# Fused decoder layer: the mirrored columns for the first join, and the place of X of level 0 in the round

## The reference, cut to what matters

```python
mixed = silu(conv4(x @ w_qkv)); z = x @ w_z          # q, k, v from mixed, q and k of unit length
def step(S, (q, k, v, g, b)):
    S = S * exp(g)
    delta = (v - k @ S) * b
    S = S + outer(k, delta)
    return S, q @ S                                   # o
on = rmsnorm(o * silu(z)) * norm_w
out = on @ w_out
```

## Time and profile before

| what | value |
|---|---|
| time, median of three runs | 3113.66 us (3106.82 to 3114.77) |
| the profiled execution | 3111.22 us, span 3109.4 us |
| mean granted TensorE clock | 0.978 |
| busy: TensorE, VectorE, ScalarE, GpSimd | 2949.2 us (95%), 2671.0 (86%), 1935.2 (62%), 634.4 (20%) |
| instructions: TensorE, VectorE | 29096, 6317 |
| DMA queue of the kernel | 454566 packets, 314.87 MB, 34.1% of 16 engines |
| from one `turn_kq` to the next | 38.7 (chunk 0), 42.9 (1), 42.5 (2), 39.8 us (3), as read in rounds 43 to 46 |

### The profile page before, as it was taken

The page is one execution under the profiler, slowest core; times in us unless marked ns, Lnnn a source line. Parts: engine busy times, 40 slices in busy tenths (PEclk is TensorE's granted clock), DMA queues, the critical chain, the costliest instruction groups (busy, mean ns, idle before and its releaser), DMA issues. The chain is left out here.

```text
span 3109.4 us, 79479 instructions
## 1 busy us (share of the span) xinstructions
PE 2949.2 (95%) x29096; PEld 2419.4 (78%) x29096; DVE 2671.0 (86%) x6317; ACT 1935.2 (62%) x6258; POOL 634.4 (20%) x911
## 2 busy tenths in 40 slices
PE   6999999999999999999999999999999999649998
PEld 3788888888888888888888888888888888536665
DVE  4798989898988889898989898889888888789984
ACT  4576666666767666666667666666676766533332
POOL 1121212121212121111212121112121211162320
PEclk9899999999999999999999999999999999859999
DMA  7433434333433343433343333333343333020000
GB/s 259 141 88 107 121 108 123 105 117 103 123 107 118 89 123 109 123 100 122 96 128 89 103 115 110 121 108 115 105 121 107 116 92 101 22 99 21 28 14 17
DMA packets 454952, 319.96 MB, mean 103 GB/s; under 512 B 244003, under 2 KB 407971, under 8 KB 436902
## 3 DMA queue, kind: packets, MB, share of 16 engines
q1 hardware_dynamic: 454566, 314.87, 34.1%
HBM read 247.26 MB, written 50.73 MB: 96 GB/s over the span
## 5 line engine op out<-in xcount | busy, mean ns | idle before, releaser
L1077 DVE SCALAR_TENSOR_TENSOR conv<-xb,convw,conv 128x512 f32<-128x512 f32 x768 | 591.6, 774 | 97.6 <-ACT conv L786 82.8
L569 PE MATMUL bank<-x_hi,w_hi 128*128 128x512 f32 x1024 | 429.4, 419 | 10.1 <-PEq L263 6.4
L569 PE MATMUL bank<-x_hi,w_lo 128*128 128x512 f32 x1024 | 402.9, 393 | 0.0
L569 PE MATMUL bank<-x_lo,w_hi 128*128 128x512 f32 x1024 | 400.2, 391 | 0.0
L780 ACT ACTIVATE xb<-bank 128x512 f32<-128x512 f32 x256 | 161.7, 632 | 302.5 <-PE bank L569 277.9
L581 PE MATMUL bank<-w_hi,x_hi 128*128 128x256 f32 x1024 | 303.1, 296 | 1.6 <-ACT conv L786 1.6
L581 PE MATMUL bank<-w_lo,x_hi 128*128 128x256 f32 x1024 | 289.6, 283 | 0.0
L581 PE MATMUL bank<-w_hi,x_lo 128*128 128x256 f32 x1024 | 289.6, 283 | 0.0
L1160 POOL TENSOR_TENSOR small<-small,half 128x4 f32<-128x4 f32 x64 | 64.5, 1008 | 1047.7 <-DVE small L904 1047.7
L1188 POOL COPY halo<-xb 128x12 f32<-128x12 f32 x256 | 93.3, 365 | 863.3 <-ACT xb L780 863.3
L569 PEld LDWEIGHTS bank<-x_hi,w_hi 128*128 128x128 f32 x1024 | 193.8, 189 | 47.4 <-issue 10.1
(11 more groups left out here) (266 smaller groups left out, 7644.5 us busy)
## 6 DMA issues: line engine op xcount, KB each, us to landing
x_hi<-x_hi_scratch SPq DMA_DIRECT2D x63, 1024.0 KB, 5.0
x_lo<-x_lo_scratch SPq DMA_DIRECT2D x63, 1024.0 KB, 8.2
E<-decay_scratch SPq DMA_DIRECT2D x64, 512.0 KB, 5.4
M_scratch<-M SPq DMA_DIRECT2D x128, 256.0 KB, 2.2
w_raw<-in_w_proj SPq DMA_DIRECT2D x64, 384.0 KB, 8.5
Mt<-M_scratch SPq DMA_DIRECT2D x256, 64.0 KB, 2.0
U<-Ut SPq DMA_DIRECT2D x256, 64.0 KB, 2.0
w_raw<-in_w_out SPq DMA_DIRECT2D x32, 256.0 KB, 2.9
```

The costliest lines, as they stand in the source:

```text
L569: mm = pe.matmul(banks[j % 2][:].rearrange("p (b t) -> p b t", b=B), lhsT=t[f"w_{p}"][:, k, j, :], rhs=t[f"x_{q}"][:, k], start=i == 0, st ...
L1077: dve.scalar_tensor_tensor(out=y3, in0=xb[:, :, i:i + C], scalar=t["convw"][:, j, i:i + 1], in1=y3, op0=ALU.mult, op1=ALU.add).then_inc(on ...
```

## The change

1. Mt. Each of the four loads L348 is cut to the 64 columns of its own half (the ones that levels 0 and 1 read). Four more loads bring, for rows q = 0 and 1, the column blocks 2 and 3 to the places 3 and 2, so that Mt's upper right part is mirrored by columns too. Together 160 instead of 96 counts of `d_M` a step.
2. `join_a` takes from Mt one product of 64 columns instead of two of 32: eight matmuls instead of twelve.
3. TensorE: `x_part(r+1, 0)` moves ahead of `gate(r+2, 2)`. VectorE: `turn_T(r+1, 0)` and `x_part(r+1, 0)` move ahead of `taps(r+2, 2)`.

```diff
-                sp.wait_ge(on["d_M"], 96 * s + 32)
+                sp.wait_ge(on["d_M"], 160 * s + 32)
...
                 for q in range(4):
-                    sp.dma_start(Mt[rows(3 - q)], M_units[rows(q), 4:8]).then_inc(on["d_M"], 16)
+                    own = slice(0, 64) if q < 2 else slice(64, 128)
+                    sp.dma_start(Mt[rows(3 - q), :, own], M_units[rows(q), 4:8, own]).then_inc(on["d_M"], 16)
+                for q in range(2):
+                    for k in (2, 3):
+                        sp.dma_start(Mt[rows(3 - q), :, rows(5 - k)], M_units[rows(q), 4:8, rows(k)]).then_inc(on["d_M"], 16)
...
-                pe.wait_ge(on["d_M"], 96 * (s + 1))
+                pe.wait_ge(on["d_M"], 160 * (s + 1))
...
                 pe.matmul(x64[hi, i], lhsT=M8[lo, i, hi], rhs=T64[lo, i, :], start=True, stop=True)
-                for q in (2, 3):
-                    mm = pe.matmul(x64[at(i + 4, q), i], lhsT=Mt[hi, i, rows(q)], rhs=T64[hi, i, :], start=True, stop=True)
+                mm = pe.matmul(x64[lo, i], lhsT=Mt[hi, i, hi], rhs=T64[hi, i, :], start=True, stop=True)
             mm.then_inc(on["XF"], 1)
...
                 gate(r + 2, 1)
+            if solve:
+                x_part(r + 1, 0)
+            if ahead:
                 gate(r + 2, 2)
-            if solve:
-                x_part(r + 1, 0)
...
                 taps(r + 2, 1, range(early, TAPS - 1))
-                taps(r + 2, 2)
             if solve:
                 turn_T(r + 1, 0)
                 x_part(r + 1, 0)
             if ahead:
+                taps(r + 2, 2)
                 taps(r + 2, 3, (0,))
```

More of the change, by code:

```diff
@@ L611, in tensor @@
                 gate(r + 2, 1)
-                gate(r + 2, 2)
             if solve:
                 x_part(r + 1, 0)
+            if ahead:
+                gate(r + 2, 2)
             if ahead:
```

## The result

The change takes the median from 3113.2 to 3096.1 us (ten runs each). The ratio of the changed kernel to the kernel before is 0.9947, with a 95% interval from 0.9922 to 0.9972: faster by 0.5%, where 0.9% was forecast. The single runs spread more than before, 3071 to 3111 us against 3106 to 3117.

What follows compares the result with a forecast made beforehand. TensorE sets the pace (busy 491 of 500 us), VectorE follows (445). Steps of -1.83 us per four rounds, 16 times, give -29; +1.4 once makes -28: 3083, or 3086 with 2.4 for the median. Range 3036 to 3119.

Steps and rivals of the forecast that it cites:

- The forecast steps: Shifts of the solve's start from each chunk's round to the next, together -1.83 us in four rounds.
- The join: `join_a` on TensorE falls from 1.95 to 0.62 us, 1.33 us less a round; ceiling 85 us in 64 rounds.
- VectorE's end hands over: At the round's end, TensorE's 1.33 us can't be taken out of any round unless VectorE's end moves too.
- a slack of 1.05 us at U: `turn_kq` of the next round waits for ScalarE's U, behind VectorE's last taps; slack 1.05 us, but 0.38 in chunk 1.
- The other hand-over, M: VectorE waits for the Gram product ahead of M, up to 0.6 us in chunks 1 and 3; lateness beyond about 0.8 delays the solve.
- Chunk 1: TensorE's 1.22 us wait for Xc goes, but VectorE's end comes only 0.33 us earlier, by its lost idle time.
- The loads at nothing: SP's four more Mt loads take about 1.9 us to issue, at no cost; 0.5 us likely enough for the range.
- the sign that I had named for a price: More than the present 5.1 us from T's save to the last of Tc's loads, and waits for Tc in all chunks.
- The new waits for Tc: About 1 us on both engines in chunks 3 and some of 0; in round 43, 1.4 us VectorE, 0.9 TensorE.
- A: Slacks at U and M don't bind, so the join's gain arrives whole: -73 us, 3041; chance 0.18.
- B: T's save or Tc's loads queue behind the later E, delaying every Tc: +10 us, 3124 at 1.2 us; chance of slower 0.14.
- C: The two joins don't overlap, `join_a` stays above 1.5 us, sum about zero: 3113; chance 0.18, shared with a gain-eating Tc delay.
- D: X earlier frees nothing since Y still waits for R from ScalarE; in chunk 1 costs 5 us of forecast; no chance given.

Runs made afterwards that it cites:

- U first: ScalarE's `join_b` ahead of v's second Silu: on the whole change 3089.6 us (0.9929); on the kernel with the moves in chunks 1 and 2 only 3057.3 us (0.9824).

## Why the prediction was right, and where not

**The number** lies within the range, at -17 us where -28 was forecast. Part of that is luck. The forecast steps for chunks 0 to 3 were -0.3, -0.33, -0.75 and -0.45 us; measured are +0.55, -1.19, -0.65 and +0.10. Chunk 2 alone came near its forecast. Chunks 0 and 3 have the wrong sign, and chunk 1 gained more than three times what I gave it.

**The join** was sized right: 0.62 us, as `join_b`. Four matmuls at the 0.12 us that I had read for one would have left it at about 1.5; I put the rest down to the tiles' width, which no longer alternates. No run changes the width and keeps the count, so this division is argued. The Trainium skill says in "TensorEngine Tiling (Array Packing)", Tiling Modes, Key Properties, that a change of the tiling mode drains TensorE; the rows agree: before, the two kinds start 0.23 to 0.26 us apart, and the matmuls of one kind now 0.06.

**That the join's gain arrives in part only** was right. 85 us of TensorE time became 31 to 33 us alone (0.9896) and 50 with the moves where they help. The reason I gave, that VectorE's end hands over, is shown for chunk 1 by U (15 waits, one in four rounds) and by what took U's place when U came earlier: another instruction at VectorE's end. For the other chunks I had read a slack of 1.05 us at U, under the 1.33; there U never shows as a wait, in no run. So in the sum the step from chunk 3 to 0 had the wrong limit: with the join alone, where TensorE waits only 5.0 us for Tc, that step is -0.56 us and not -1.05. The other hand-over, M, was used up as forecast: VectorE's waits for the Gram product go from 43 to 15. TensorE's and VectorE's waits for R, N and Y are there instead; which of them holds a round is not settled by these runs.

**Chunk 1** was sized too small. I counted 0.33 us of VectorE's idle time; the moves alone take 0.71 us off this chunk (42.88 to 42.17), and the join's share comes on top. Where the rest comes from was not followed.

**The loads at nothing** was right for the loads by themselves. But the sign that I had named for a price is there in part: in round 43, from T's save to the last of Tc's issues, 5.7 us against 5.1, and in chunk 0 Tc comes 0.9 us later in the round with the loads alone. What that adds to the new waits is not measured.

**The new waits for Tc** were placed right: VectorE's are in chunks 3 and 0 alone, and so are 40.2 of TensorE's 41.1 us (the two others, of 0.49 and 0.37 us, are in chunks 1 and 2). They were put too small. In chunks 0 and 3 the join alone gained 0.75 and 0.56 us; with the waits and the drops behind them both got longer. Their size: I had 0.9 us on TensorE for round 43 and found 1.77:

```profile
1896.84 0.45 PE L431 MATMUL bank<-Tc,M 32*32 32x32 f32 x32 [1.77 <-issue]
```

In that round SP needed 6.2 us from T's save (1889.25) to the end of Tc's issues, against 5.5 before; over the 56 steady rounds the mean is 5.2 against 5.0, and in chunk 0 5.5 against 4.7. In chunk 0 it is the longer way, then. In chunks 1 to 3 it is T's save itself, which stands 0.8 to 1.0 us later behind the start of its round than before (19.4 to 20.0 us against 18.5 to 19.1), and VectorE now waits for N there too.

**The clock** is the term that was missing. I counted a microsecond of waiting as a microsecond. Eight times TensorE went to half its clock for 3.41 us behind such a wait, which cost 1.3 us more, 10 us together. With them the forecast of -28 us would have been -18, against -17.1 measured between the medians. That the two agree so closely is luck, as the steps of the single chunks show.

**The rivals.** A (the gain whole, 3041) has no support: even with the waits of TensorE for Tc down to 5.0 us the time stays at 3057. B as I put it (waits for Tc in all chunks, and slower) did not come; a small part of its mechanism did, as said for the loads. C is refuted by the 0.62 us. D was that Y waits for R anyway. The moves alone take 0.71 us off chunk 1, so D does not hold there; X earlier does free nothing when TensorE's half is moved alone, but for another reason, since Xc comes late.

## What to carry to other kernels

Before a product is moved ahead in the order of an engine that never idles, read for each kind of round when its input lands, not only for the round that the move is meant for: here the same move is worth 0.6% where the input landed over 2 us before (chunks 1 and 2, half of it from drops of the clock that go) and costs 1.1% where it is the last to come, and a condition on the round keeps the first without the second (3060 us against 3096). A gain on the busiest engine is worth no more than the next engine's end lets through; read the slack at each hand-over to the next round, and then check by a run whether it is the one that binds. Products on parts of the TensorE array are worth keeping at one tile width in a row: four matmuls less and no change of width made 1.95 us into 0.62. And time that costs nothing where it falls into a slack, like the later Tc of the new loads, has to be counted again when another part of the change uses that slack.

## What the runs showed of the hardware that I had not expected

TensorE's granted clock fell to 0.50 for 3.41 us behind single waits in rounds that were otherwise full. In the changed kernel all eight drops came behind waits of 1.81 to 2.21 us for Tc, but two others of its ten waits in that range had none:

```profile
1084.81 0.45 PE L431 MATMUL bank<-Tc,M 32*32 32x32 f32 x32 [1.93 <-issue]
2586.81 0.45 PE L431 MATMUL bank<-Tc,M 32*32 32x32 f32 x32 [1.90 <-issue]
```

Shorter waits were enough elsewhere: 1.68 us in the kernel with the moves alone, and this one in the kernel with TensorE's move in all chunks, 1.3 us before a drop at 1410.5:

```profile
1409.15 0.45 PE L431 MATMUL bank<-Tc,M 32*32 32x32 f32 x32 [1.53 <-issue]
```

The kernels with the moves in chunks 1 and 2 and with x_part in mid-gate had waits of up to 1.7 us and no drop. So the length of one wait does not decide by itself, and what does is not settled here. Two shorter waits close together can do the same. In the kernel with the join alone TensorE idled 1.10 us for R and 1.21 us for Xc within 3 us, and the clock fell at about 1000 us:

```profile
996.83 0.63 PE L543 MATMUL bank<-eye,R 128*128 128x128 f32 x4 [1.10 <-ACT R L755]
998.67 0.75 PE L449 MATMUL bank<-Xc,Uc 32*32 32x32 f32 x64 [1.21 <-DVE Xc L990]
```

```profile
1000.00:1001.00 1.00, 1.00 (x6) 1.00 (x6) 0.90 (x2) 0.00 (x0) 0.00 (x0) 0.50 0.07 16
```

The number of drops in rounds 1 to 60, in the one profiled execution of each kernel:

| kernel | drops |
|---|---|
| before; the loads alone | 0 |
| the whole change | 8 |
| the whole change with U first | 6 |
| join alone; moves alone | 6; 5 |
| TensorE's move in all chunks, VectorE's in 1 and 2 | 6 |
| TensorE's move in 1 and 2, VectorE's in all; VectorE's in none | 0; 3 |
| moves in 1 and 2, without and with U first; x_part in mid-gate | 0 |

The runs of the changed kernel spread over 40 us between the lowest and the highest of ten, against 11 before. The mean granted clock of each run goes with its time: 0.976 in the fastest (3071 us), 0.970 and 0.971 in the three slowest (3103 to 3111 us), and 0.973 to 0.975 in the others. So the number of drops probably differs from run to run; that they cause the spread was not tested.
